# A two-layer kernel: the skip term as a diagonal product, the gate on VectorE, loads and parts further ahead, layer 0's sum by tokens

## The reference

```python
# layer 0
xn = layernorm(x)
x = x + mla_attention(xn) + ffn(xn)     # attention over the 16 heads of one token, bias bout at its end
# layer 1
xn = layernorm(x)
h  = rmsnorm(xn) * norm_w
u, z = split(h @ in_proj_w)             # 256 channels each
u  = silu(causal_conv4(u) + conv_b)
dt_r, Bm, Cm = split(u @ x_proj_w)      # 64, 16, 16
dt = softplus(dt_r @ dt_proj_w + dt_proj_b)
hst[t] = exp(dt[t] * A) * hst[t-1] + dt[t] * Bm[t] * u[t]     # 256 channels x 16 states
y  = einsum(hst, Cm) + u * D            # the skip term
y  = y * silu(z)                        # the gate
x = x + xn + y @ out_proj_w + moe(xn)   # moe: 1 shared and 8 routed experts, the best 2 of each token
```

## Time and profile before

| | us |
|---|---|
| median of three runs | 1319.91 |
| lowest, highest | 1317.92, 1344.87 |
| the profiled execution | 1330.25 |
| its span from first to last instruction | 1328.1 |
| busy: TensorE matmul, VectorE, GpSimd (POOL), ScalarE | 911.6, 943.1, 709.4, 505.4 |

### The profile page before, as it was taken

One profiled execution on the slowest core, in us unless ns is written; L12 is line 12 of the kernel. 1 busy time (PEld: TensorE's weight loads), 2 busy tenths in 40 slices (PEclk: granted clock), 3 DMA queues, 4 the chain that ended last, 5 costly groups with the idle time before them and its releaser, 6 DMA issues. The chain is left out here.

```text
span 1328.1 us, 12681 instructions
## 1 busy us (share of the span) xinstructions
PE 911.6 (69%) x3460; PEld 416.8 (31%) x3460; DVE 943.1 (71%) x1288; ACT 505.4 (38%) x842; POOL 709.4 (53%) x547
## 2 busy tenths in 40 slices
PE   4677877977768535447867876876886877754553
PEld 1222322322223211113534433543444534421110
DVE  3577786776867450157878788798689788789884
ACT  1112212312123111255556465474564565562320
POOL 1012102101064305635856666678688888779996
PEclk9668878779588666667987888997886887985655
DMA  4984664646431204366666666676785776655641
GB/s 138 217 173 112 149 177 130 154 137 149 106 108 35 70 24 148 85 160 194 158 159 174 156 174 171 179 182 162 162 212 162 165 180 175 193 137 129 140 123 28
DMA packets 102833, 192.23 MB, mean 145 GB/s; under 512 B 13259, under 2 KB 68108, under 8 KB 90348
## 3 DMA queue, kind: packets, MB, share of 16 engines
q1 hardware_dynamic: 91500, 183.00, 53.0%
q0 software_dynamic: 11264, 8.43, 3.6%
HBM read 146.74 MB, written 32.06 MB: 135 GB/s over the span
## 5 line engine op out<-in xcount | busy, mean ns | idle before, releaser
L1459 POOL TENSOR_TENSOR hc<-hs,c_rep 128x512 f32<-128x512 f32 x256 | 368.9, 1530 | 159.3 <-DVE hs L1723 158.7
L1716 DVE TENSOR_TENSOR p_du<-p_du,b_rep 128x512 f32<-128x512 f32 x256 | 175.4, 685 | 107.8 <-PE p_du L1834 107.7
L1834 PE MATMUL p_du<-block_in,spread 96*128 96x512 bf16 x256 | 116.6, 460 | 156.9 <-DVE hs L1723 126.5
L1723 DVE TENSOR_TENSOR_SCAN hs<-slots,p_du 128x512 f32<-128x512 f32 x128 | 156.3, 1221 | 14.3 <-POOL hc L1459 3.2
L1723 DVE TENSOR_TENSOR_SCAN hs<-decays,p_du 128x512 f32<-128x512 f32 x128 | 156.3, 1221 | 14.2 <-POOL hc L1459 2.7
L447 POOL TENSOR_TENSOR sc<-ex,ex_part 128x1024 f32<-128x1024 f32 x8 | 17.0, 2128 | 214.2 <-ACT ex_part L535 214.2
L679 DVE TENSOR_TENSOR value_prod<-p_eb,v 128x512 f32<-128x512 f32 x128 | 83.7, 684 | 46.4 <-PE p_eb L959 46.0
L1495 POOL DMA_INDIRECT y_xr<-moe_sums,position x64 | 104.9, 1640 | 16.3 <-issue 14.0
L1834 PEld LDWEIGHTS p_du<-block_in,spread 96*128 96x128 bf16 x256 | 26.1, 103 | 276.8 <-DVE hs L1723 200.2
L1591 ACT ACTIVATE decays<-decays,a_neg 128x512 f32<-128x512 f32 x128 | 87.5, 719 | 40.6 <-DMA decays<-dt_rows 40.6
L1843 PE MATMUL p_y<-hc,gather 128*32 128x512 f32 x512 | 84.8, 741 | 22.4 <-POOL hc L1459 22.4
(11 more groups left out here) (186 smaller groups left out, 1711.9 us busy)
## 6 DMA issues: line engine op xcount, KB each, us to landing
qb<-rq_rows SPq DMA_DIRECT2D x32, 1024.0 KB, 13.4
decays<-dt_rows SPq DMA_DIRECT2D x32, 1024.0 KB
slots<-dt_rows SPq DMA_DIRECT2D x32, 1024.0 KB
wm<-in_wmoe SPq DMA_DIRECT2D x48, 384.0 KB
moe_rows<-zeros SPq DMA_DIRECT2D x8, 774.0 KB, 6.4
xg<-moe_rows SPq DMA_DIRECT2D x48, 129.0 KB, 14.0
stack<-ex_part SPq DMA_DIRECT2D x96, 64.0 KB
block_in<-y_part SPq DMA_DIRECT2D x192, 32.0 KB
```

The lines of the kernel that those rows point to most:

```text
L1459: nc.gpsimd.tensor_tensor(hc[:, k % NA], hs[:, k % 4], c_rep[:, p], ALU.mult).then_inc(hc_done.sem, 1)
L1716: nc.vector.tensor_tensor(p_du[:, k % 2], p_du[:, k % 2], b_rep[:, p], ALU.mult).then_inc(dbu_done.sem, 1)
L1723: nc.vector.tensor_tensor_scan(hs[:, k % 4], decays[(8 * (b - 1) + k // 4) % NQ][:, bass.ts(j, T)], p_du[:, k % 2], 0.0, ALU.mult, ALU.add ...
L1834: nc.tensor.matmul(p_du[:, k % 2], spread[:, i], block_in[:, s, j], start=True, stop=True).then_inc(du_full.sem, 1)
```

## The change

**Layer 0.** `project_out` makes the sum with tokens on the partitions: for each of four blocks of 128 tokens, attention and the three hidden blocks are the stationary operand and the weights the moving one, in 16 products of 128 columns. `copy_sum` and `turn_back` go. The bias is added to `x` by POOL (`add_bias`, one batch ahead), and `add_up` waits for `project_out` and for it. `choose(0)`, `place(0)`, `ranks(0)` and the scatters of the first half move one round later; the logits of all eight batches have places of their own.

**Layer 1.** TensorE begins each half of `p_y` with a product of `u` with a diagonal matrix of D; VectorE's `skip` goes and VectorE does `gate_y` from `p_y`, POOL does not. `softplus_one` moves from VectorE to ScalarE (`one_more`). Both halves' parts are made and stacked a batch ahead, in three buffers of `block_in`. `decay` runs 3 steps ahead. Rows are loaded 14 steps ahead of their unit and weights 12, with 5 buffers of weights and 3 of results, and a tile is stored 4 steps behind it. `load_decays` stands one step later in SP's list.

```diff
             def add_up(b):
-                dve.wait_ge(back_full.sem, back_full.at(b))
+                dve.wait_ge(acc_full.sem, acc_full.at(b))
+                dve.wait_ge(biased.sem, biased.at(b))
...
+            def add_bias(b):
+                if b == 1:
+                    pool.wait_ge(loaded0, 16 * n_small)
+                pool.wait_ge(ln_done.sem, ln_done.at(b))
+                nc.gpsimd.tensor_tensor(x[:, (b - 1) % NX], x[:, (b - 1) % NX], bout[:].unsqueeze(1).to_broadcast([128, TT, D]), ALU.add)\
+                    .then_inc(biased.sem, 1)
...
             for b in range(1, B + 3):
                 if 1 <= b - 2 <= B:
                     second_root(b - 2)
+                if b == 1:
+                    add_bias(1)
+                if b < B:
+                    add_bias(b + 1)
                 if b <= B:
                     first_rest(b)
...
-                if b == 7:
+                if b == B:
                     send(0, 0)
-                if b == 8:
+                if b == B + 1:
                     send(0, 1)
...
-                nc.tensor.matmul(p_acc[:], wout[:], attn[:], start=True, stop=False)
-                for f in range(FT0):
-                    ins = nc.tensor.matmul(p_acc[:], wd[:, f], hid[:, f], start=False, stop=(f == FT0 - 1))
+                for t in range(TT):
+                    nc.tensor.matmul(p_acc[:, bass.ts(t, D)], attn[:, bass.ts(t, 128)], wout[:], start=(t == 0), stop=False)
+                    for f in range(FT0):
+                        ins = nc.tensor.matmul(p_acc[:, bass.ts(t, D)], hid[:, f, bass.ts(t, 128)], wd[:, f],
+                                               start=False, stop=(t == TT - 1 and f == FT0 - 1))
...
                 if b + 2 <= B:
                     turn_x(b + 2)
                     latent(b + 2)
-                if old:
-                    turn_back(b - 1)
...
-        NR = 4
+        NR = 5
         NX = 6
+        NO = 3
+        NB = 3
         NQ = 4
+        AHEAD = 3
...
-                    for _, _, j, v in due(b, k, 11):
+                    for _, _, j, _ in due(b, k, 14):
                         if j is not None:
-                            load_tile(j, v)
-                    if new and k % 4 == 1 and k < 20:
-                        load_decays(b, (k + 11) // 4)
-                    if nxt and k % 4 == 1 and k > 20:
-                        load_decays(b + 1, (k - 21) // 4)
-                    if new and k in (6, 8, 9):
-                        stack(b, 1, (6, 8, 9).index(k))
-                    for _, _, j, _ in due(b, k, -2):
+                            load_rows(j)
+                    for _, _, j, _ in due(b, k, 12):
+                        if j is not None:
+                            load_weights(j)
+                    if new and k % 4 == 2 and k < 20:
+                        load_decays(b, (k + 10) // 4)
+                    if nxt and k % 4 == 2 and k > 20:
+                        load_decays(b + 1, (k - 22) // 4)
+                    for _, _, j, _ in due(b, k, -4):
                         if j is not None:
                             store_tile(j)
...
                         if k in (21, 22, 23):
                             stack(b + 1, 0, k - 21)
+                        if k in (25, 26, 27):
+                            stack(b + 1, 1, k - 25)
...
-                    if old and k == 4:
-                        gate_y(b - 1, q, 1)
-                    if new and k == 20:
-                        gate_y(b, p, 0)
...
+            def one_more(b):
+                act.wait_ge(sp_exp.sem, sp_exp.at(b))
+                act.wait_ge(part3.sem, part3.at(b - 1))
+                nc.scalar.activation(wz, ez, ACT.Copy, bias=1.0).then_inc(sp_one.sem, 1)
...
-            def skip(b, p, s):
+            def gate_y(b, p, s):
                 dve.wait_ge(gathered.sem, gathered.at(b, 4 * s + 4))
-                dve.wait_ge(y_done.sem, y_done.at(b, s) if s else y_done.at(b - 1))
-                nc.vector.scalar_tensor_tensor(y1[:], u[:, p, s], w["d_skip"][:, s:s + 1], p_y[:], ALU.mult, ALU.add)\
-                    .then_inc(y1_done.sem, 1)
+                if s == 0:
+                    dve.wait_ge(acc_full.sem, acc_full.at(b - 1))
+                    dve.wait_ge(z_done.sem, z_done.at(b))
+                nc.vector.tensor_tensor(yt[:, s], p_y[:], sz[:, p, s], ALU.mult).then_inc(y_done.sem, 1)
...
-                    if new and k == 6:
-                        second_rest(b, 1)
-                    if new and k == 8:
-                        third_part(b, 1)
...
-                    if k == 14:
-                        softplus_one(b + 1)
                     if k == 15:
                         softplus_cut(b + 1)
-                    if k == 17:
+                    if k == 16:
                         softplus_end(b + 1)
-                    if k == 20:
-                        second_rest(b + 1, 0)
-                    if k == 22:
-                        third_part(b + 1, 0)
+                    if k in (20, 24):
+                        second_rest(b + 1, (k - 20) // 4)
+                    if k in (22, 26):
+                        third_part(b + 1, (k - 22) // 4)
...
                 if q % 4 == 0:
-                    pe.wait_ge(y1_done.sem, y1_done.at(b, q // 4) if q else y1_done.at(b - 1))
+                    pe.wait_ge(y_done.sem, y_done.at(b, q // 4) if q else y_done.at(b - 1))
+                    pe.wait_ge(u_done.sem, u_done.at(b))
+                    nc.tensor.matmul(p_y[:], skip[:, q // 4], u[:, p, q // 4], start=True, stop=False)
```

182 lines of the change are left out of this document (84 added, 98 removed).

## The result

The changed kernel takes 1265.76 us (median of four runs, 1260.48 to 1278.65), the kernel before beside it 1318.91 us: a ratio of 0.9616, 95% interval 0.9522 to 0.9711. That is faster by more than 2%, inside the range of 1212 to 1285, and 21 us above the forecast; the forecast's second case, *given back* at 1270, lies closest. The profiled execution took 1278.65 us, the slowest of the four, against 1330.25: 51.6 us less where the sum had 74.4.

The account below looks back on a forecast made before the run. No engine is full: VectorE's work plus its waits sets the time until 1170 us, then POOL's final chain. Terms sum to 74.4 us off the profiled 1330.25, less 10.3 for the median: 1245 us, range 1212 to 1285.

Parts of the forecast that it names:

- given back: Rival, chance 0.20: waits end but other engines in the same lists hold the time; a third of the gain goes, 1270.
- Layer 0, `add_up`: Layer 0: VectorE's waits ahead of `add_up` mostly go, 25.6 us saved (bounds 12 to 29.3), 2.1 of round 9's 5.23.
- `add_bias`: Layer 0, rounds 3 to 7: POOL's addition slows VectorE's normalization of `x1` by 0.86 us each, +4.3 (bounds 0 and 8.6).
- Scatters a round later: Layer 0, round 8: VectorE's wait for the root behind the scatters goes, 3.4 us saved (bounds 0 and 3.4).
- Rows of the experts: Layer 1: rows get 7 steps to land instead of 4, cutting VectorE's `p_du` waits; 30 us saved (bounds 20 and 35).
- The end: Last stretch: POOL loses `gate_y`, 5.3 us saved (bounds 2 and 6); the 5.21 us before the first gather stay.
- `softplus_one`: Layer 1: leaves VectorE in six batches with its waits, 13.7 us saved (bounds 10 and 14); ScalarE adds an activation.
- Parts and stacking: Layer 1: a `block_in` wait goes, 1.1 us (bounds 0, 20); half 1's parts leave k=6 and 8, 5.6 (0, 14).
- The diagonal product: Layer 1, TensorE: at k=22 it stands ahead of `spread_du`; six cost about 1 us each, +6.0 (bounds 0 and 18).
- no real change: Rival, chance 0.08: rows stay late behind transfers ahead in SP's queue, layer 0 gives back half, product costs 18; 1300.
- The clock: Rival, chance 0.15: fewer waits keep TensorE's clock high; 4 us in each of five rounds, 5 in the batches; 1220.
- Slower: Rival, chance 0.04: SP blocks on new, earlier waits for results, so decays load late and scans wait; up to 1377.

Follow-up runs that it names:

- The run with five loads of weights: Changed kernel with only the first five loads of experts' weights, 43 transfers and their waits left out, results wrong; 1253.49 us, ratio 0.9473.
- The last run: Changed kernel without the diagonal product, first gathers of batches 4 and 7 later, each half's last tile stored two steps behind; 1238.62 us, ratio 0.9393.
- the profile of layer 0 alone: Layer 0 of the changed kernel with layer 1 of the kernel before, no other edit; 1297.62 us, ratio 0.9830.

## Why the prediction was right, and where it was wrong

The time lies in the stated range because the range was wide enough for a large miss: it lies above the forecast's own 1232 to 1260. Layer 0 (27.1 of 24.7 us) and the end (8.0 of 5.3) came as forecast; the batches gave 16.6 of 44.4.

**Layer 0, `add_up`: right.** 27.7 + 1.6 us of waits became 6.2, so 23.1 went of the 25.6 forecast. The step for round 9 was wrong in direction: the copy and the transposes left, but VectorE still waits 5.56 us for the product, not 3.1.

**`add_bias`: right in size, wrong in place.** It is not the normalization that the addition meets (that takes 1.1 us as before) but the short product of the two roots ahead of it (L735), which takes 0.85 us instead of 0.16 in rounds 3 to 7: 3.5 us, forecast 4.3. In round 5 POOL's addition ends at 221.64 + 1.27 = 222.91 and the product at 222.08 + 0.85 = 222.93: VectorE waits for what is left of POOL's instruction. That is how the Trainium skill, page "SBUF — State Buffer", section "Who interferes with whom", has it for a VectorE instruction with both inputs in SBUF. The trace agrees; the price was a remainder of an addition, not a whole one.

**Scatters a round later: smaller.** The 3.40 us of round 8 went, but in round 9 the root is now behind 16 scatters and VectorE waits 8.95 us for it. All waits for the root come to 13.2 us before and 10.7 after: 2.5 saved of 3.4.

**Rows of the experts: the step that failed first.** That the rows' wait would go was right: 46.1 us became none. What failed is "they had 4 steps and now have 7", taken as if nothing else in the queue moved. The rows land as late as before (median 14.5 us; before 14.0, but the trace tells the landing of only 8 of those 48 loads, so the earlier trace rows is thinner than the prediction took it for), the weights' wait rose from 3.7 to 24.2 us, and with the 26.0 for `xgt` TensorE waits 50.2 us for its experts' inputs where it waited 51.0. The forecast saw `softplus_one` as covered. On VectorE it is, but on ScalarE the row that it lengthens holds the copy `xgt` for 4 to 6 us a batch. "SP's list keeps its length" was true of the list and not of the time, since issuing the same 144 transfers took 180.7 us instead of 94.3; what that costs is not shown. The run with five loads of weights shows that most of the idle time (109.5 - 62.2 = 47.3 us) is behind the transfers. Taking the earlier loads back costs 12.9 us of waits for `p_du` and 6 to 12 us of the stretch by the profiles, where the term had 30 with 20 as its lower bound; the times alone, 30 us give or take 17, would allow it. The rest of the 26.6 us by which `p_du` fell belongs to the other moves, and the runs do not divide it.

**The end: one half right, the other the second failure.** The last stretch fell by 8.0 us, 7.3 of them `gate_y` (forecast 5.3). But "the 5.21 us ahead of the first gather stay about as they are" was wrong. The forecast looked at the start of the chain that ended last and not at the other first gather, in batch 4, and took two steps more for harmless. POOL's waits are 15.06 us there and 10.6 ahead of batch 7's, 25.7 in all, and they cost VectorE 16.9 us of waiting, three fifths of the shortfall of 27.8. `softplus_end` beside POOL's catching up costs 4.5 more. The last run takes most of this away and gets 20.8 us back, by both ways.

**`softplus_one`: right.** It took 12.3 us of VectorE's work with it, and L1691's wait of 4.0 has become one of 1.4 for the sum. What the forecast did not have is that `softplus_end`, moved from k=17 to k=16 with it, grew by 5.2 us.

**Parts and stacking: cannot be said.** The steps show 0.4 us a batch where the forecast had 0.8, and `block_in` is waited for no more. New waits of VectorE for the parts come to 3.9 us. The times say that undoing it costs 0.029 of the time with an interval of about 0.02 either way, which the steps do not explain.

**The diagonal product: under the forecast as work, open in its place.** By the medians the six at k=22 cost half a us each and the seven steps 7 are 0.7 us longer than without it, 8 us where the forecast had 6.0. But undisturbed batches are of one length with none, one and two of them, so other steps give this back. What its place costs in the others is open, as said above.

**The rivals.** *Given back* named the right size, and that is luck, for its reason is wrong: it is mostly not the engines' lists that hold the time but the transfers, as *no real change* had it for the rows. *The clock* came in layer 0 only, and small. From 577.3 and 550.2 to batch 8 it is 0.83 and 0.85. In layer 0, from `add_up` of round 2 to that of round 6 (207.0 us before, 188.1 after), it rose from 0.83 to 0.89, and VectorE's waits ahead of `value_prod` fell from 23.8 to 18.9 us, on top of the 16.7 for `add_up`. In the profile of layer 0 alone, with the same layer 0, the clock is 0.82, these waits are 22.5 us and the stretch 192.3. So some 4 of the 27.1 us go with the clock, where the rival had 20; that layer 0 as a whole came out so near its 24.7 is in part luck. *Slower*, SP blocking on new earlier waits, had the place right (SP, and decays behind it) and the mechanism wrong: SP's waits for results fell, and its issuing grew. Of the signs named in advance, new waits for `wm` came. ScalarE's for the decays became more, not new: 19.0 us in two waits in the middle stretch before, 25.9 in ten after.
